# Perceiver layer with routed experts: at the end GpSimd takes every fourth token tile of the final sum

## The reference

```
topw, topi = jax.lax.top_k(probs, TOP_K)
topw = topw / jnp.sum(topw, axis=-1, keepdims=True)
combine = jnp.einsum('tk,tke->te', topw, onehot)
gate = jax.nn.silu(jnp.einsum('th,eih->eti', xf, w_gate))
up = jnp.einsum('th,eih->eti', xf, w_up)
down = jnp.einsum('eti,ehi->eth', gate * up, w_down)
out = jnp.einsum('eth,te->th', down, combine)
...
x = x + _L0_ffn_ref(_layernorm(x, axis=-1), ...)
```

## Time and profile before

| | |
|---|---|
| median of 3 runs | 480.22 us (479.7 to 482.32) |
| the profiled execution's own time | 479.78 us |
| its span | 477.9 us |
| from the first load of `Y` (L274) to the end of the span | 463.81 to 477.9 us |
| VectorE's work in the tail | 467.74 to 475.12 us |
| granted TensorE clock, mean | 0.964 |

### The profile page before, as it was taken

One profiled execution on the slowest core, in us unless ns is written; L12 is line 12 of the kernel. 1 busy time (PEld: TensorE's weight loads), 2 busy tenths in 40 slices (PEclk: granted clock), 3 DMA queues, 4 the chain that ended last, 5 costly groups with the idle time before them and its releaser, 6 DMA issues. The chain is left out here.

```text
span 477.9 us, 13886 instructions
## 1 busy us (share of the span) xinstructions
PE 419.8 (88%) x4037; PEld 338.5 (71%) x4037; DVE 321.6 (67%) x954; ACT 296.4 (62%) x875; POOL 206.0 (43%) x482
## 2 busy tenths in 40 slices
PE   0889999999999999999988799988977999999950
PEld 0567677777767777777756687887876888888850
DVE  5368888888888888888875678888471333333325
ACT  3588888888888888888875878742122232232234
POOL 0545555545555454555531100000005777777740
PEclk9999999999999999999999999999579999999995
DMA  5345111111111111111000000001007766766626
GB/s 159 78 152 202 37 42 33 44 33 38 39 33 44 33 38 38 33 43 33 11 2 1 0 2 1 1 1 67 23 7 245 216 201 212 217 189 216 185 63 240
DMA packets 31999, 38.86 MB, mean 81 GB/s; under 512 B 5952, under 2 KB 29184, under 8 KB 31712
## 3 DMA queue, kind: packets, MB, share of 16 engines
q1 hardware_dynamic: 29472, 33.35, 22.8%
q0 software_dynamic: 2496, 5.12, 3.6%
HBM read 33.80 MB, written 4.65 MB: 80 GB/s over the span
## 5 line engine op out<-in xcount | busy, mean ns | idle before, releaser
L398 ACT ACTIVATE PR<-PS,nmax 128x257 f32<-128x257 f32 x256 | 117.9, 474 | 30.5 <-DVE nmax L586 30.5
L586 DVE TENSOR_REDUCE nmax<-PS 128x1 f32<-128x257 f32 x256 | 90.5, 416 | 20.0 <-PE PS L861 19.9
L868 PE MATMUL PS<-I,PR 128*128 128x128 f32 x512 | 67.3, 275 | 0.0
L348 POOL DMA_INDIRECT XG<-x_table,IDX x39 | 37.8, 970 | 58.1 <-DVE IDX L789 46.5
L868 PEld LDWEIGHTS PS<-I,PR 128*128 128x128 f32 x512 | 58.7, 143 | 0.3 <-issue 0.3
L302 POOL TENSOR_TENSOR O<-OM 128x64 f32<-128x64 f32 x64 | 20.4, 319 | 84.1 <-DVE OM L609 84.1
L795 DVE TENSOR_TENSOR H<-PS,SG 128x384 f32<-128x384 f32 x39 | 21.7, 558 | 49.9 <-PE PS L1081 48.8
L398 ACT ACTIVATION_READ_ACCUMULATOR PR<-PS,nmax 128x1 f32 x256 | 51.9, 203 | 0.0
L529 ACT ACTIVATE SG<-PS 128x384 f32<-128x384 f32 x39 | 19.1, 490 | 49.5 <-PE PS L1081 49.5
L883 PE MATMUL PS<-PT,KV 128*32 128x128 f32 x1024 | 41.6, 280 | 6.2 <-DVE PT L591 5.8
L861 PE MATMUL PS<-KV,QM 32*128 32x257 f32 x512 | 45.8, 427 | 1.3 <-ACT PR L398 0.7
(11 more groups left out here) (194 smaller groups left out, 837.7 us busy)
## 6 DMA issues: line engine op xcount, KB each, us to landing
CR<-ctxT SPq DMA_DIRECT2D x64, 128.0 KB, 2.1
GC<-w_gate SPq DMA_DIRECT2D x39, 192.0 KB
UC<-w_up SPq DMA_DIRECT2D x39, 192.0 KB, 3.4
Y<-y_table SPq DMA_DIRECT2D x4, 512.0 KB, 5.2
DW<-w_down SPq DMA_DIRECT2D x1, 1536.0 KB, 6.1
NAMES<-lanes SPq DMA_DIRECT2D x1, 1344.0 KB, 8.3
X<-x SPq DMA_DIRECT2D x4, 256.0 KB, 3.5
x_table<-xe SPq DMA_DIRECT2D x4, 256.0 KB, 2.4
```

What stands on the lines that cost most here:

```text
L348: g.indirect_dma_start(XG[:, s % XRING, :], None, x_table[:, :], bass.IndirectOffsetOnAxis(IDX[:, s:s + 1], 0)).then_inc(gathered[s % XRIN ...
L398: a.activation(PR[:, j % 2, gr, 0:S], src, ACT.Exp, bias=bias, accum_out=rsum[:, j % 2, gr:gr + 1]).then_inc(exped, 1)
L586: v.tensor_reduce(nmax[:, gr:gr + 1], bank[gr][:, 0:S], AX.X, ALU.max, negate=True).then_inc(max_ready, 1)
L868: ins = t.transpose(bank[4 + ch][:, 128 * gr:128 * gr + 128], PR[:, j % 2, gr, KC * ch:KC * ch + KC], I128[:, :])
```

## The change

GpSimd does the whole sum of the tiles 3, 7, 11 and 15, in three instructions a tile: it scales the first row in place, adds it to `X`, then adds the second row, which ScalarE has scaled. A new semaphore `fourth` counts these instructions; each waits for the one before it through that semaphore. VectorE does three tiles a group in place of four, and its final addition is 128x384 in place of 128x512. ScalarE does the same 16 scalings, but in each group the fourth tile first. SyncE waits for `fourth` as well before it stores a group.

```
             for n in range(4):
                 sp.wait_ge(c["out"], n + 1)
+                sp.wait_ge(c["fourth"], 3 * n + 3)
                 sp.dma_start(out[512 * n:512 * n + 512, :].rearrange("(t p) d -> p t d", p=128), X[:, 4 * n:4 * n + 4, :]).then_inc(stored, 16)
...
+            g.wait_ge(c["w_out"], 2)
+            for n in range(4):
+                m = 4 * n + 3
+                g.wait_ge(in_y[n], 16)
+                g.tensor_scalar(Y[:, m, 0, :], Y[:, m, 0, :], WT[:, 0, m:m + 1], None, ALU.mult).then_inc(c["fourth"], 1)
+                g.wait_ge(c["fourth"], 3 * n + 1)
+                g.tensor_tensor(X[:, m, :], X[:, m, :], Y[:, m, 0, :], ALU.add).then_inc(c["fourth"], 1)
+                g.wait_ge(c["fourth"], 3 * n + 2)
+                g.wait_ge(c["second"], 4 * n + 1)
+                g.tensor_tensor(X[:, m, :], X[:, m, :], Y[:, m, 1, :], ALU.add).then_inc(c["fourth"], 1)
...
-            for m in range(T):
-                if m % 4 == 0:
+            for m in (4 * n + k for n in range(4) for k in (3, 0, 1, 2)):
+                if m % 4 == 3:
                     a.wait_ge(in_y[m // 4], 16)
                 a.activation(Y[:, m, 1, :], Y[:, m, 1, :], ACT.Copy, scale=WT[:, 1, m:m + 1]).then_inc(c["second"], 1)
...
             for n in range(4):
-                s = slice(4 * n, 4 * n + 4)
+                s = slice(4 * n, 4 * n + 3)
                 v.wait_ge(in_y[n], 16)
-                for m in range(4 * n, 4 * n + 4):
+                for m in range(4 * n, 4 * n + 3):
                     v.scalar_tensor_tensor(out=X[:, m, :], in0=Y[:, m, 0, :], scalar=WT[:, 0, m:m + 1], in1=X[:, m, :],
                                            op0=ALU.mult, op1=ALU.add).then_inc(c["summed"], 1)
-                v.wait_ge(c["summed"], 4 * n + 4)
+                v.wait_ge(c["summed"], 3 * n + 3)
                 v.wait_ge(c["second"], 4 * n + 4)
                 v.tensor_tensor(X[:, s, :], X[:, s, :], Y[:, s, 1, :], ALU.add).then_inc(c["out"], 1)
```

More of the change, by code:

```diff
@@ L178, in build @@
             "owners", "chosen", "named", "valued", "rowed", "listed", "silu_set", "ids", "second", "w_out", "x_stored", "xg_turned", "xg_copied",
-            "gate", "up", "silu", "hidden", "down", "ys", "summed", "out")}
+            "gate", "up", "silu", "hidden", "down", "ys", "summed", "fourth", "out")}
         gathered = [sem(f"gathered{n}") for n in range(XRING)]
```

## The result

The changed kernel takes 486.91 us (median of 6 runs, 485.44 to 488.09), the kernel before 480.61 us (6 runs, 479.7 to 482.87); the ratio is 1.0105, 95% interval 1.0078 to 1.0133. Forecast was 481.0 us in a range of 478.3 to 483.2. The profiled execution took 486.85 us with a span of 485.0, 7.1 us more than before.

A forecast was written before the change was run, and what follows sets the result against it. VectorE was taken as the bound from 469.10 us on. Its saving of 1.33 us and SyncE's 0.06 gave 478.5 without interference; with turns while reading, 1.24 later plus 0.06 on 479.78 gave 481.0, range 478.3 to 483.2.

The forecast's parts named there:

- The step that failed: End of program: moves one for one with the last group's sum; 1.88 us outside the span fixed.
- The slow one: VectorE and GpSimd in the tail: whole instructions exclude each other, 482.6 us, up to 483.5; chance 0.26.
- something unseen: Anywhere in the kernel: a cause the prediction doesn't see, no size given; chance 0.05.
- The turns while reading: VectorE and GpSimd in the tail: overlap in fixed parts, alternate SBUF reads; 2.15 us a group, 481.0 us; chance 0.42.
- GpSimd's own sum: GpSimd's share of the tail, alone: scaling 0.37 us, each addition 0.453, a group 1.38.
- VectorE's part: VectorE's groups in the tail: period from 1.77 to 1.375 us, last addition ending 1.33 us earlier.
- ScalarE's and SyncE's parts: Tail: ScalarE's reordered scalings change nothing; SyncE's extra wait adds 0.06 us on the last store.
- The sign that the prediction set itself: Stretch up to 467.7 us: untouched, so a move over 0.5 us would make the prediction wrong as a whole.

The follow-up runs named there:

- The late mark: The kernel before with one GpSimd MEMSET of 128x1 added that waits until VectorE's last group is summed; ratio 1.0085 (1.0046 to 1.0124).

## Why the prediction was wrong

**The step that failed** is in its first part: "the rest of the span and 1.88 us outside it are fixed. The end of the program moves one for one with the end of the last group's sum." The rest of the span was fixed only as long as GpSimd was done early.
```profile
461.16 0.26 POOLq L41
```

The prediction asked who waits for GpSimd, answered SyncE's stores, and left out the common end, so this term stood at nothing. The late mark shows +3.9 us from this alone, the run without the drain the reverse.

**No rival had it.** The slow one (482.6, up to 483.5) was the right direction for another reason, and the range left the measured value out by 3.7 us at its upper end. The shape of the forecast failed with it: the chances of 0.77 for no change and 0.20 for slower rested on a sum over the two engines alone, and 0.05 was left for something unseen.

**The turns while reading** were right in kind and too large. 2.15 us a group was forecast, 1.88 came; the end of the last sum moved by +0.50 us, not +1.24. VectorE lost 0.51 us a group (1.89 against 1.38 without GpSimd's share), not 0.73, and GpSimd 0.23 (1.88 against 1.65 alone), not 0.80: they got in each other's way at some readings, not at every one. In the changed kernel's groups after the first, VectorE's three SCALAR_TENSOR_TENSORs took 0.54, 0.45 and 0.34 us (0.34 each alone) and its addition 0.75 (0.56 alone); of GpSimd's three instructions only the second addition is clearly longer, 0.65 for 0.45. By the Trainium skill, "SBUF — State Buffer", section "Who interferes with whom", a VectorE instruction with two SBUF inputs contends with a GpSimd instruction that reads SBUF, not with one that only writes; the runs agree on both halves, 0.75 against 0.56 us for the addition with GpSimd's arithmetic and with its MEMSETs. The rule of an exclusive lock held for whole instructions, in its section "SBUF: two separate sides", would have made the two engines' works add up. The runs don't agree: alone a group takes VectorE 1.38 us and GpSimd 1.65, 3.03 in a row, and together both were through in 1.88, with single losses of 0.1 to 0.2 us, 0.33 at most (0.78 for 0.45, in the first group).

**GpSimd's own sum** was right for the additions (0.453 worked out, 0.45 measured alone) and wrong for TENSOR_SCALAR: 0.37 taken between 0.29 and 0.453, 0.60 measured alone. I bounded it with a two-input operation from above, and an operand that is one scalar for each partition isn't of that kind. What it moved in the result can't be told apart from the interference: GpSimd ended last, at 478.32, 0.31 us behind VectorE.

**VectorE's part** was right: 1.375 us a group worked out, 1.38 measured without GpSimd. **ScalarE's and SyncE's parts** were right, as far as seen: VectorE's first addition still waits for ScalarE, and the stores land 2.3 us after their issue.

**The sign that the prediction set itself.** It called itself wrong as a whole if the stretch up to the first landing moved by more than 0.5 us. It moved by 2.7 (467.64 to 470.34). That sign can't serve: the kernel before, unchanged, took 477.5 to 484.9 us in 69 executions beside the experiments.

**The remainder between the runs and the tail.** The medians differ by 6.3 us and the ratio of the runs says 5.0 (3.8 to 6.4), where the tails say 4.3. Much of that spread goes with the mean granted clock of TensorE. The six executions of the changed kernel had 0.955 to 0.959. Of those 69 of the kernel before, whose clocks go from 0.955 to 0.973, the 12 with 0.955 to 0.959 have a median of 483.3 us; against them the changed kernel's 486.91 is 3.6 us more, within 0.7 of the 4.3 of the tail. The change as such doesn't seem to lower the clock: without the end drain, the same instructions had a mean of 0.962 in 12 executions, as the 23 of before beside them. Why these six executions had a low clock stays open, and with it the exact size of the loss outside the tail, if there is one.
